# A two-layer GRU with a mixture of experts: one PSUM bank for each gate, transposed one by one, and mixture products in two calls of 128 columns

## What is computed

```python
# block 1: x + out, a GRU of two layers over 1024 steps
mixed = tanh(x @ W_in.T + b_in + ctx)
xg = h_below @ Wih.T + bih                 # for each layer
hg = h @ Whh.T + bhh                       # at each step
r = sigmoid(xr + hr); z = sigmoid(xz + hz); n = tanh(xn + r * hn)
h = (1 - z) * n + z * h
out = (gate * h2 + h2) @ W_out.T + b_out
# block 2: x + (shared + routed) / 3
shared = silu(x @ w1) * (x @ w3) @ w2
s = sigmoid([x, cond] @ router_W)          # the best 2 of 8 experts, normalised
routed = sum_e combine_e * (gelu(x @ W1e[e]) @ W2e[e])
```

## Time and profile before

| what | value |
|---|---|
| median of 3 runs | 2193.89 us |
| lowest and highest run | 2191.0 and 2194.55 us |
| span of the profiled execution | 2185.8 us |
| time beside the span (median less span) | 8.1 us |
| PE: busy, matmuls | 2068.4 us, 69,920 |
| DVE: busy, instructions | 1841.5 us, 11,225 |
| ACT: busy, instructions | 1201.4 us, 6,471 |
| instructions fetched by queue q8 | 548 packets, 8.98 MB |

### The profile page before, as it was taken

The page is one execution under the profiler, slowest core; times in us unless marked ns, Lnnn a source line. Parts: engine busy times, 40 slices in busy tenths (PEclk is TensorE's granted clock), DMA queues, the critical chain, the costliest instruction groups (busy, mean ns, idle before and its releaser), DMA issues.

```text
span 2185.8 us, 162058 instructions
## 1 busy us (share of the span) xinstructions
PE 2068.4 (95%) x69920; PEld 1485.0 (68%) x69920; DVE 1841.5 (84%) x11225; ACT 1201.4 (55%) x6471; POOL 560.5 (26%) x2542
## 2 busy tenths in 40 slices
PE   6989899999999999999999999999999999999987
PEld 3666666677666776767767676666767676777766
DVE  4888889888888888888888888888888888888874
ACT  2555555555555555555555555555555555555542
POOL 1222232222322223222222222222232222222220
PEclk9999999999999999999999999999999999999999
DMA  5000000000000000000000000000000000000000
GB/s 219 4 4 5 4 5 5 24 5 5 9 5 24 5 5 10 5 24 5 10 5 24 5 5 9 5 24 5 5 10 5 24 5 10 5 21 9 5 16 19
DMA packets 10879, 32.76 MB, mean 15 GB/s; under 512 B 1368, under 2 KB 6832, under 8 KB 9136
## 3 DMA queue, kind: packets, MB, share of 16 engines
q1 hardware_dynamic: 10160, 22.38, 2.8%
HBM read 20.22 MB, written 2.16 MB: 10 GB/s over the span
## 4 chain that ended last, share of the span: by engine, by line
PE 60%; DVE 26%; ACT 10%; issue 3%; DMA 1%; SPq 0%; POOL 0%; DVEq 0%; POOLq 0%
PE bank L333 29%; PE bank L325 17%; PE bank L272 11%; DVE n_first L404 9%; DVE cells L424 7%; ACT factors L472 6%; ACT cells L476 4%; DVE r_pre L395 4%; DVE z_pre L405 3%; PE bank L306 3%; DVE bank L413 1%; DVE n_second L380 0%; DVE x L687 0%; PE bank L657 0%; DVE hid L745 0%
## 5 line engine op out<-in xcount | busy, mean ns | idle before, releaser
L333 PE MATMUL bank<-w_h,cells 128*22 128x128 f32 (+4 forms) x32768 | 1363.4, 281 | 23.6 <-DVE cells L424 13.9
L333 PEld LDWEIGHTS bank<-w_h,cells 128*22 128x22 f32 (+4 forms) x32768 | 853.0, 111 | 130.5 <-DVE cells L424 91.3
L325 PEld LDWEIGHTS bank<-w_h,cells 128*2 128x2 f32 (+15 forms) x28112 | 512.2, 113 | 528.1 <-DVE cells L424 502.8
L517 POOL TENSOR_SCALAR cells<-cells 128x4 f32<-128x4 f32 x2048 | 463.6, 226 | 1525.8 <-DVE cells L424 1524.8
L325 PE MATMUL bank<-w_h,cells 128*2 128x64 f32 (+15 forms) x28112 | 770.1, 225 | 76.3 <-DVE cells L424 55.5
L466 ACT ACTIVATE n_second<-r_pre 128x4 f32<-128x4 f32 x2048 | 426.3, 208 | 508.8 <-DVE r_pre L395 466.3
L472 ACT ACTIVATE factors<-z_pre 128x4 f32<-128x4 f32 x2048 | 429.6, 210 | 436.5 <-DVE z_pre L405 358.8
L404 DVE STREAM_TRANSPOSE n_first<-bank 128x64 f32<-128x64 f32 x2048 | 600.0, 293 | 33.1 <-PE bank L333 23.7
L424 DVE TENSOR_TENSOR_SCAN cells<-factors,cells 128x18 f32<-128x18 f32 x2048 | 397.2, 194 | 241.5 <-ACT cells L476 177.1
L395 DVE STREAM_TRANSPOSE r_pre<-bank 128x64 f32<-128x64 f32 x2048 | 480.6, 235 | 33.3 <-PE bank L325 24.9
L405 DVE STREAM_TRANSPOSE z_pre<-bank 128x64 f32<-128x64 f32 x2048 | 427.4, 209 | 0.0
(11 more groups left out here) (91 smaller groups left out, 558.8 us busy)
## 6 DMA issues: line engine op xcount, KB each, us to landing
c_all<-weights SPq DMA_DIRECT2D x6, 1024.0 KB
x_t<-in_x_t SPq DMA_DIRECT2D x4, 512.0 KB, 7.4
w_1e<-in_w_1e SPq DMA_DIRECT2D x1, 2048.0 KB
w_2e<-in_w_2e SPq DMA_DIRECT2D x1, 2048.0 KB
w_x<-in_w_x SPq DMA_DIRECT2D x2, 768.0 KB, 8.2
w_h<-in_w_h SPq DMA_DIRECT2D x2, 768.0 KB, 9.5
w<-in_w SPq DMA_DIRECT2D x3, 512.0 KB
out_y<-y SPq DMA_DIRECT2D x6, 256.0 KB, 3.5
```

The costliest lines, as they stand in the source:

```text
L325: mm = pe.matmul(r_sums[l][p][32 * g:32 * g + B * (j + 1)], state_tile(l, j, kt), w_h[l][:, kt, g, 2 * U:], start=False, stop=False, tile_ ...
L333: mm = pe.matmul(sums[l][p][32 * g:32 * g + B * (j + 1), 0:width], state_tile(l, j, kt), w_h[l][:, kt, g, 0:width], start=False, stop=Fals ...
L517: pool.tensor_scalar(cell_part(step_rows(l, j), 3), cell_part(step_rows(l, j), 1), 0.5, None, ALU.mult)\
```

## The change

**Banks.** Bank 0 holds the r sums of both layers and both sets, bank 1 those of n, bank 2 those of z. Bank 3 holds the `sums` of both layers, one set for each, and only the projections and biases go there.

**A step.** `recur` now makes each gate by a call of `gate_sums`: 8 calls of 64 columns for r, 8 for n, 8 for z, in every step. Before n it waits until DVE has transposed z of the step that came before on PE, the other layer's (semaphore `turn`), since n and z of both layers share a bank each. DVE waits for each gate by itself, and transposes r of layer 1 ahead of layer 0's scan.

**Once in a chunk.** DVE copies three parts out of `sums` (`fill_r`, `fill_n`, `fill_z`) instead of one, between the transposes, in the slots that `fills_next` names. The wait for the biases moves from the fourth step to the projection.

**The mixture.** In windows of 128 slots a product is cut in two of half as many columns (`mix.cuts`), each with a half-slot of its own, and PE takes them in both parts of a slot.

```diff
@@ -33,17 +32,14 @@
-def places_biases(t):
-
-    return CH <= t < T - CH
-
-
-def r_first(l, t):
-
-
-
-    s = t + LAG * l
-    return s % CH not in ((0, 4, 8, 12) if s >= SHORT else (4, 12))
+def places_biases(l, t):
+
+    return t < T - CH and t % CH == 3 + l
+
+
+def fills_next(l, s):
+
+    return s % CH == 13 and s < T - CH if l == 0 else s % CH == 1 and CH <= s < T + CH
...
-            return j in projection_pieces(part ^ 1) or part == 1 and (self.sparse or self.window > 5 * CH and j % 8 != 6)
+            return j in projection_pieces(part ^ 1) or part == 1 and 5 * CH < self.window < GROUPS[0] and j % 8 != 6
         if engine == "act":
-            return ((j - LAG) if part else j) % CH == 2 or self.sparse and part == 1
-        return (j, part) in ((13, 0), (1, 1), (2, 1))
+            return (j, part) in ((3, 0), ((4 + LAG) % CH, 1)) or self.sparse and part == 1
+        return (j, part) in ((13, 0), (1, 1))
...
-        r_sums = [[banks[l][:, p * U:(p + 1) * U] for p in range(2)] for l in range(2)]
-        sums = [[banks[2 + l][:, p * NGATE * U:(p + 1) * NGATE * U] for p in range(2)] for l in range(2)]
+        r_sums, n_sums, z_sums = ([[bank[:, (2 * l + p) * U:(2 * l + p + 1) * U] for p in range(2)] for l in range(2)] for bank in banks[0:3])
+        sums = [banks[3][:, l * NGATE * U:(l + 1) * NGATE * U] for l in range(2)]
...
+        def gate_sums(pe, at, l, j, first):
+
+            for kt in range(KT):
                 for g in range(NQ):
...
-            if r_first(l, t):
-                for kt in range(KT):
-                    for g in range(NQ):
-                        mm = pe.matmul(r_sums[l][p][32 * g:32 * g + B * (j + 1)], state_tile(l, j, kt), w_h[l][:, kt, g, 2 * U:],
-                                       start=False, stop=False, tile_position=(0, 32 * g), skip_group_check=True)
-                mm.then_inc(s["r"], 1)
-            if j == 3 and places_biases(t):
-                pe.wait_ge(s["bias"], 1)
-            width = 2 * U if r_first(l, t) else 3 * U
-            for kt in range(KT):
-                for g in range(NQ):
-                    mm = pe.matmul(sums[l][p][32 * g:32 * g + B * (j + 1), 0:width], state_tile(l, j, kt), w_h[l][:, kt, g, 0:width],
-                                   start=False, stop=False, tile_position=(0, 32 * g), skip_group_check=True)
-            mm.then_inc(s["pe"], 1)
+            at = t + LAG * l
+            other, slot = (at - 1 - LAG, at - 1) if l == 0 else (at, at)
+            if l == 1 and t == 0:
+                pe.wait_ge(sets[0][other // CH % 2]["turn"], 2 * (other % CH) + 1)
+            gate_sums(pe, r_sums[l][p], l, j, 2 * U).then_inc(s["r"], 1)
+            if 0 <= other < T:
+                pe.wait_ge(sets[1 - l][other // CH % 2]["turn"], 2 * (other % CH) + 2)
+            gate_sums(pe, n_sums[l][p], l, j, 0).then_inc(s["n_pe"], 1)
+            if fills_next(1 - l, slot):
+                pe.wait_ge(sets[1 - l][slot // CH % 2]["xn"], 1)
+            gate_sums(pe, z_sums[l][p], l, j, U).then_inc(s["pe"], 1)
...
-            if t >= 0:
-                pe.wait_ge(sets[l][p]["turn"], 2 * (t % CH) + 2)
-            mm = project_all(pe, l, 1 - p, kt)
+            mm = project_all(pe, l, kt)
...
+        def fill_n(v, l, p):
+
+            v.tensor_copy(n_sums[l][p], sums[l][:, 0:U])
+
+        def fill_z(v, l, p):
+
+            v.tensor_copy(z_sums[l][p], sums[l][:, U:2 * U]).then_inc(sets[l][1 - p]["xn"], 1)
...
+        def dve_turn_n(v, l, t):
+
+            p, j = t // CH % 2, t % CH
+            s = sets[l][p]
+            v.wait_ge(s["n_pe"], j + 1)
+            v.transpose(n_first[l][:, :, :, 2].rearrange("p i b -> p b i"), blocks(n_sums[l][p])).then_inc(s["for_n"], 1)
...
-                c, j = divmod(s, CH)
-                p = c % 2
-                if t0 is not None and r_first(0, t0):
+                q = 1 - s // CH % 2
+                fills = [fills_next(l, s) for l in range(2)]
+                if t0 is not None:
                     dve_turn_r(v, 0, t0)
+                if fills[0]:
+                    v.wait_ge(sets[0][1 - q]["x"], 1)
+                    fill_r(v, 0, q)
                 if 0 <= s - 1 - LAG < T:
                     dve_h(v, 1, s - 1 - LAG)
-                if t0 is not None and not r_first(0, t0):
-                    dve_turn_r(v, 0, t0)
                 if t0 is not None:
-                    dve_turn_nz(v, 0, t0)
+                    dve_turn_n(v, 0, t0)
+                if fills[0]:
+                    fill_n(v, 0, q)
+                if t0 is not None:
+                    dve_turn_z(v, 0, t0)
+                if fills[0]:
+                    fill_z(v, 0, q)
+                if t0 is not None:
                     dve_n(v, 0, t0)
-                    if j == 13 and t0 < T - CH:
-                        v.wait_ge(sets[0][p]["x"], 1)
-                        take_r(v, 0, 1 - p)
-                        take_n(v, 0, 1 - p)
+                if fills[0]:
+                    take_n(v, 0, q)
                 mixture_at(v, "dve", s, 0, base)
+                if t1 is not None:
+                    dve_turn_r(v, 1, t1)
+                if fills[1]:
+                    v.wait_ge(sets[1][1 - q]["x"], 1)
+                    fill_r(v, 1, q)
+                if fills[1] and t1 is None:
+                    fill_n(v, 1, q)
+                    fill_z(v, 1, q)
                 if t0 is not None:
                     dve_h(v, 0, t0)
                 if t1 is not None:
-                    dve_turn_r(v, 1, t1)
-                    dve_turn_nz(v, 1, t1)
+                    dve_turn_n(v, 1, t1)
+                    if fills[1]:
+                        fill_n(v, 1, q)
+                    dve_turn_z(v, 1, t1)
+                    if fills[1]:
+                        fill_z(v, 1, q)
                     dve_n(v, 1, t1)
-                if CH <= s < T + CH and j == 1:
-                    v.wait_ge(sets[1][p]["x"], 1)
-                    take_r(v, 1, 1 - p)
-                if CH <= s < T + CH and j == 2:
-                    take_n(v, 1, 1 - p)
+                if fills[1]:
+                    take_n(v, 1, q)
...
-            if j == 2 and places_biases(t):
-                act.activation(sums[l][1 - p], biases[l][:], ACT.Identity).then_inc(s["bias"], 1)
+            if places_biases(l, t):
+                act.activation(sums[l], biases[l][:], ACT.Identity).then_inc(s["bias"], 1)
...
+            TC, CUT = TG // len(mix.cuts), mix.cuts[-1]
+
+            def cut(c):
+                return slice(TC * c, TC * c + TC)
+
...
+                    for c in mix.cuts:
+                        for kt in range(KT):
+                            if kind == "s":
+                                w = feature_tile((w_1, w_3)[h][:, kt], i)
+                            else:
+                                w = feature_tile(w_1e[:, i, kt], h)
+                            mix.add("pe", f"up{u}_{h}{c}{kt}", free if h == kt == c == 0 else (),
+                                    product(ups[u % 2][:, h, cut(c)], w, x2[:, kt, cut(c)], h == kt == c == 0, kt == KT - 1))
```

More of the change, by code:

```diff
@@ L21 @@
 LAG = CH + 3
-SHORT = 56 * CH
 ELT = 4
@@ L68, in __init__ @@
         self.pieces = range(2 if steps > 5 * CH else 1)
+        self.cuts = self.pieces if self.sparse else range(1)
         self.y_done = f"y{KT - 1}{self.pieces[-1]}"
@@ L293, in place_biases, with project_all @@
         def place_biases(pe, l):
-            for p in range(2):
-                for g in range(NQ):
[L297 to L304, removed]
-            for g in range(NQ):
-                mm = pe.matmul(sums[l][p][32 * g:32 * g + 32, U:], stage[l][:, kt, :], w_x[l][:, kt, g, :],
-                               start=False, stop=False, tile_position=(0, 32 * g), skip_group_check=True)
+            for g in range(NQ):
+                strip = slice(32 * g, 32 * g + 32)
+                pe.matmul(sums[l][strip], ones[:, :], w_b[l][:, g, :], start=l == 0, stop=False,
+                          tile_position=(0, 32 * g), skip_group_check=True)
+                for p in range(2):
+                    for at in (r_sums, n_sums, z_sums):
+                        mm = pe.matmul(at[l][p][strip], ones[:, :], w_b[l][:, g, 0:U], start=l == p == 0, stop=False,
+                                       tile_position=(0, 32 * g), skip_group_check=True)
+            mm.then_inc(s_bps, 1)
+        def project_all(pe, l, kt):
+            for g in range(NQ):
+                mm = pe.matmul(sums[l][32 * g:32 * g + 32, U:], stage[l][:, kt, :], w_x[l][:, kt, g, :],
+                               start=False, stop=False, tile_position=(0, 32 * g), skip_group_check=True)
+            return mm
+        def gate_sums(pe, at, l, j, first):
+            for kt in range(KT):
+                for g in range(NQ):
+                    mm = pe.matmul(at[32 * g:32 * g + B * (j + 1)], state_tile(l, j, kt), w_h[l][:, kt, g, first:first + U],
```

(23 more changed lines are left out.)

61 lines of the change are left out of this document (30 added, 31 removed).

## The result

The changed kernel takes 3259.59 us (median of 4 runs, 3255.48 to 3263.69) against 2193.92 us for the kernel before: a ratio of 1.486, 95% interval 1.484 to 1.488. Its profiled execution has a span of 3254.2 us. The forecast was 3247 us.

The account below looks back on a forecast made before the run. PE's instruction fetch was taken as the bound after the change: 862 packets x 3.7 us = 3189, plus 58 us (50 for start and end, 8.1 for median less span) = 3247 us, range 2954 to 3523 us.

Parts of the forecast that it names:

- The bound: PE's instruction queue: a packet of 256 instructions is needed every 3.99 us in the kernel before; fetching hidden, next to nothing to spare.
- The two parts taken from it: PE's instruction queue: edge crossing to next packet's start, 1.14 to 1.26 us; packet's start to PE going on, 2.22 to 2.28.
- The count: PE's instruction queue after the change: 111,092 matmuls, as many weight loads and 450 others make 870 packets, 548 before.
- The time of one: Fetch time of one instruction packet on PE: taken as 3.7 us, the middle between 3.36 and 4.02.
- The 8.1 us for what lies around the span: Whole kernel: median time less profiled span, 8.1 us, added to the packets' time in the forecast.
- The array's work and the new waits: PE's gates and mixture: three sets take 0.72 us against 0.68; n's wait for z's transpose costs nothing more behind the fetch.
- DVE and ACT: DVE's 256 new copies cost at most 64 us, hidden under the fetch; other DVE and ACT busy times change under 5%.
- Fetching keeps up: First rival, PE's instruction queue: prefetch feeds 256 instructions in 2.3 us, a step takes 0.99 us, 2156 us; 7 in 100.
- overlap in part: Second rival, PE's instruction queue: the 1.2 us before a packet runs beside the transfer, 2200 us; 4 in 100.
- The same weights are loaded once: Third rival, gates' weight loads on PE: two of three dropped, 614 packets remain, 2300 us; 1 in 100.
- The gain of 38 us: Step loop if fetching were free: 33 us from shorter steps and about 5 at the ends, 2194 to 2156 us.
- takes it off the loop: DVE's order: transposing layer 1's r ahead of layer 0's state scan removes 0.12 us or so between that scan and n.

## Why the prediction was right

**The bound.** Fetching was read as hidden with next to nothing to spare, from two rows of "issue" and the count of weight loads between them. The changed kernel shows the same mechanism at 838 stops for 869 packets. One reading was of an odd case: the stop in the earlier trace rows was lengthened by the 1 MB load ahead of it. The two parts taken from it, 1.14 to 1.26 and 2.22 to 2.28 us, lie within what all stops after show (1.04 to 1.81 and 2.2 to 3.0), so nothing was lost by it.

**The count.** 870 packets were worked out and 869 are there; matmuls are 111,092 as worked out. The start and the end have 164 and 800 matmuls against the 204 and 772 of the earlier trace rows:

```profile
0.00:20.00 20.00, 13.02 (x164) 1.00 0.85 287
3224.00:3254.00 30.00, 24.34 (x800) 1.00 0.11 31
```

**The time of one.** 3.7 us was a choice between 3.36 and 4.02, and 3.72 is what the result gives (3.71 by the 673 packets in 2500 us). That it lay in the range was worked out; that the middle came within 0.02 is luck. The 12.6 us between 3247 and 3259.6 are 0.015 us a packet. The 8.1 us for what lies around the span were in the main a difference between runs: after the change the profiled execution took 3255.96 us with a span of 3254.2. Two stops in a row at 3.75 and 3.47 us lie inside the bounds; the part from crossing to the packet's start was put at 1.14 to 1.26 us and is 0.90 to 1.09 in the rows after.

**The array's work and the new waits, costed at nothing behind the fetch.** Right in sum: the run with three sets and the one with whole products differ in all of the waits and by 10 us. The wait for `turn` is seen in the profile (99.5 us, 395 times) and does not move the time beyond that.

**DVE and ACT.** For the 256 new copies 64 us were allowed. All copies into the gates' banks take 83.9 us (lines 377, 381, 385), against 27.3 before (line 376), so 57 us came. DVE's busy time rose by 116. The rows of the transposes rose by 118 us (z from 209 to 249 ns, r from 235 to 249; z's is no longer issued right behind n's without a wait, which may be why), those of the two scans fell by 120, and since rows overlap on the engine the other 59 us are not told apart. It is hidden, like the rest. One sign failed: ACT's busy time was to change by under 5% and fell by 10%, from 1201.4 to 1078.4 us, which was not looked into and costs nothing here. The rate of the state scan was put at 1.55 us and is 1.54 to 1.61.

**The rivals.** "Fetching keeps up" falls by the rows and by three runs with a known number of packets; "overlap in part", 2200 us, falls with it. "The same weights are loaded once" falls by the count of 869. The gain of 38 us that the first rival gave the new order if fetching were free is not confirmed or denied in size. The pair with half the products has 123 us, for all the rest of the change together. One step of the prediction was wrong and hidden: layer 1's r ahead of layer 0's scan "takes it off the loop", 0.12 us or so, but it gave nothing when it was tried alone.

**What stays open.** That the next packet is asked for only when the sequencer crosses into the one before it is read from starts of packets, at 835 of 838 stops, and no run varied how far ahead PE may fetch. Why the period takes values such as 3.47, 3.75 and 4.02 us was not looked into. What holds the kernel before beside the fetch, PE's work or one layer's round, is open too.

## What to carry to other kernels

Count the instructions of each engine and divide by the packets that its queue fetched: small matmuls with a weight load each can be free for the array and still be paid for, here 3.7 us for 256. Stops marked "issue" in the middle of a set, 256 instructions apart, say that the limit is near; from there on each further instruction costs its share of a packet, and splitting work for overlap must be paid from instructions saved elsewhere. Wider calls save instructions, but their weight loads lie bare, so the trade has to be timed.

## What was not expected of the hardware

A product of 256 columns over 128 rows of output keeps PE for 0.43 us as four calls of 32 rows, 0.58 us as two of 64, and 0.63 us as one of 128; one weight load of them takes 110, 135 and 188 ns in the mean. At the limit the time hardly depends on the program: four kernels with 811 to 869 packets, with PE busy from 2252 to 2585 us, come to 3.72 to 3.74 us a packet. A load of 1 MB can hold up the packet that PE waits for: six stops of 2.37 to 3.69 us, three in each of the two kernels, stand behind one. And a slot's time did not follow the sum of DVE's chain: taking a transpose out of it changed the time by under 0.2%.
